# Two attentions and two expert feed forwards on one core: the feed forwards computed by routed slots, 85 tiles each, with gates and scatters placed inside the attentions

## The reference

```python
x = x + attn_a(_layernorm(x), ...)   # 8 heads of 128, relative positions, over all 1024 keys
x = x + ffn(_layernorm(x), ...)
x = x + attn_b(_layernorm(x), ...)   # 16 heads of 8 with one shared key and value head, causal
x = x + ffn(_layernorm(x), ...)      # the same weights again
```

```python
gate_scores = softmax(einsum('btd,ed->bte', x, Wg))
topk_val, topk_idx = top_k(gate_scores, 2)
topk_val = topk_val / (topk_val.sum(-1) + 1e-9)
comb = (one_hot(topk_idx, 8) * topk_val[..., None]).sum(-2)   # 4 x 1024 x 8, two entries per token not zero
for e in range(8):
    h = einsum('btd,hd->bth', x, W1[e]) + b1[e]               # 128 -> 512
    a, b = split(h, 2, axis=-1)
    eo = einsum('bth,dh->btd', a * sigmoid(b), Wo) + bo       # 256 -> 128, Wo and bo shared by the experts
    out = out + eo * comb[..., e:e+1]
```

## Time and profile before

| | |
|---|---|
| time, median of 3 runs | 2801.4 us (2800.65 to 2802.06) |
| profiled execution | 2800.0 us, span 2798.3 us, mean granted clock 0.967 |
| PE busy | 2620.7 us, 94% of the span |
| PEld busy | 2042.4 us, 73% |
| DVE busy | 2037.5 us, 73% |
| ACT busy | 1656.8 us, 59% |
| POOL busy | 385.7 us, 14% |
| chain that ended last | PE 80%, DVE 11%, ACT 5% |

### The profile page before, as it was taken

How to read it: one execution, slowest core, us unless ns; L and a number is a source line. 1 busy time by engine, 2 the same in 40 slices (tenths; PEclk the granted TensorE clock), 3 DMA queues, 4 the chain that set the end, 5 groups by cost and what they waited for, 6 DMA issues and landing times.

```text
span 2798.3 us, 45154 instructions
## 1 busy us (share of the span) xinstructions
PE 2620.7 (94%) x14496; PEld 2042.4 (73%) x14496; DVE 2037.5 (73%) x5225; ACT 1656.8 (59%) x3430; POOL 385.7 (14%) x813
## 2 busy tenths in 40 slices
PE   4999999999999999999999889989998989988998
PEld 3788788888888888888888667755555555545776
DVE  4677766767767777677776678878777777773887
ACT  3566666666666666665666445536666656655454
POOL 1000000000000000000110233402222212222344
PEclk8999999999999999999999989969999999998999
DMA  3665566566665666656666000000000000000000
GB/s 125 226 220 200 181 224 210 192 211 208 210 211 198 210 211 209 209 206 210 226 233 209 10 1 1 1 1 1 1 1 1 1 1 1 1 1 1 9 9 16
DMA packets 97587, 321.63 MB, mean 115 GB/s; under 512 B 11924, under 2 KB 25620, under 8 KB 97140
## 3 DMA queue, kind: packets, MB, share of 16 engines
q1 hardware_dynamic: 92650, 312.84, 32.6%
q0 software_dynamic: 1584, 4.33, 0.5%
q10 hardware_dynamic: 3120, 1.57, 0.2%
HBM read 158.53 MB, written 157.29 MB: 113 GB/s over the span
## 4 chain that ended last, share of the span: by engine, by line
PE 80%; DVE 11%; ACT 5%; issue 3%; POOL 1%; DMA 0%; SPq 0%; DVEq 0%; ACTq 0%; POOLq 0%
PE ps L243 8%; PE ps L245 7%; PE ps L244 7%; PE ps L630 7%; PE ps L743 5%; PE ps L605 5%; PE ps L604 5%; PE ps L781 5%; PE ps L643 4%; PE ps L645 4%; PE ps L644 4%; PE ps L763 4%; PE ps L675 4%; PE ps L676 4%; PE ps L677 4%
## 5 line engine op out<-in xcount | busy, mean ns | idle before, releaser
L910 ACT ACTIVATE a_Ph<-ps 128x512 fp32r<-128x512 f32 x512 | 305.9, 597 | 467.8 <-PE ps L630 467.7
L1215 DVE CUSTOM_DVE_ANT_0 a_sp<-ps,a_sp 128x1024 f32<-128x1024 f32 x256 | 313.2, 1223 | 180.0 <-PE ps L245 175.9
L980 ACT ACTIVATE r_P<-ps 128x512 f32<-128x512 f32 (+3 forms) x768 | 327.9, 491 | 187.1 <-PE ps L763 182.8
L1221 DVE TENSOR_TENSOR a_Pl<-ps,a_Ph 128x512 fp32r<-128x512 f32 x512 | 349.2, 682 | 10.0 <-ACT a_Ph L910 9.8
L604 PE MATMUL ps<-a_fa,a_ua 128*128 128x384 f32 (+2 forms) x960 | 327.2, 353 | 19.3 <-DVE a_fb L1176 13.9
L931 ACT ACTIVATE r_y<-ps 128x256 f32<-128x256 f32 x512 | 194.6, 385 | 216.6 <-PE ps L677 212.4
L903 ACT ACTIVATE a_sp<-a_sp,a_nm 128x1024 f32<-128x1024 f32 x256 | 295.0, 1152 | 32.1 <-DVE a_nm L1215 31.4
L630 PE MATMUL ps<-ident,a_sp 128*128 128x128 f32 x2048 | 309.0, 273 | 0.0
L743 PE MATMUL ps<-r_K,r_Q 128*128 128x512 f32 (+3 forms) x768 | 282.5, 403 | 18.2 <-DVE r_mx L1366 12.8
L630 PEld LDWEIGHTS ps<-ident,a_sp 128*128 128x128 f32 x2048 | 250.8, 141 | 61.7 <-issue 0.6
L605 PE MATMUL ps<-a_fb,a_ub 86*128 86x384 f32 (+2 forms) x960 | 290.8, 318 | 0.0
(11 more groups left out here) (217 smaller groups left out, 5676.0 us busy)
## 6 DMA issues: line engine op xcount, KB each, us to landing
scr<-a_rt SPq DMA_DIRECT2D x256, 576.0 KB, 3.1
a_sp<-scr SPq DMA_DIRECT2D x256, 512.0 KB, 4.4
a_wc<-wsp SPq DMA_DIRECT2D x24, 512.0 KB, 5.5
wsp<-a_wc SPq DMA_DIRECT2D x8, 512.0 KB, 5.6
a_ub<-a_ua SPq DMA_DIRECT2D x64, 44.0 KB
a_w1st<-in_w1t POOLq DMA_DIRECT2D x8, 256.0 KB, 4.6
out<-x SPq DMA_DIRECT2D x4, 512.0 KB, 3.2
a_w1r<-in_w1r POOLq DMA_DIRECT2D x8, 254.0 KB, 4.4
```

The source lines that it names most:

```text
L910: e.activation(self.Ph[:, n % 3, :], ps[:, 4 + n % 2, :], ACT.Copy).then_inc(S["p_hi"], 1)
L980: e.activation(self.P[:, pt, off:512], ps[:, bank, off:512], ACT.Exp).then_inc(S["b_exp"], 1)
L1215: e.tensor_tensor_reduce(out=w, in0=ps[:, 2:4, :].rearrange("p a n -> p (a n)"), in1=w, scale=-1.0, scalar=3e38, op0=ALU.add, op1=ALU.min, ...
L1221: e.tensor_tensor(self.Pl[:, n % 3, :], ps[:, 4 + n % 2, :], self.Ph[:, n % 3, :].bitcast(F32), ALU.subtract).then_inc(S["p_lo"], 1)
```

## The change

Each token is given two *slots*, one for each of its experts. The batches are taken in three parts, `PARTS = ((0, 1), (2,), (3,))`; within a part the slots of an expert stand together and are padded to whole tiles of 128, so that a part has `PT` = 39, 23 and 23 tiles whatever the routing is, 85 in a feed forward. They are loaded in groups of four tiles. The units are:

- `m_rank` for a batch, nine fp32 matmuls of 8 to 72 columns in one bank, and `m_slot` for a part, a chain of some 12 to 18 small instructions on VectorE: they count the tokens of each expert and give the slot of each token (`m_slot`) and the expert of each tile (`m_mapi`).
- `m_disp` for a token tile: VectorE makes the normalised row tile `m_xd` (two buffers), and GpSimd issues two indirect DMAs that scatter its 128 rows to their slots in a DRAM table `xsd`.
- `m_load` and `m_turn` for a group: SyncE loads four slot tiles, TensorE transposes them (L726), ScalarE and VectorE make the high and the low part.
- `m_mm` for a slot tile: TensorE reads the expert's number from memory into a register (once for up to eight tiles) and does the three matmuls against the weights that the register picks, over banks 0 to 3; ScalarE makes the hyperbolic tangent (the sigmoid in another form), VectorE the gated product `m_gg`; there is no factor for the token's weight here.
- `m_store` for two slot tiles: SyncE stores them to a DRAM table `gsd`. `m_gath` for a token tile: GpSimd issues two indirect DMAs that gather its rows of both experts into `m_gb` (three buffers). `m_sum`, `m_fin`, `m_proj`: the weighted sum of the two, its transposition and projection, the way out as before. `m_bias` adds bo times the sum of a token's weights to x, which stood in the way out before.

`plan_a` gets the gates, ranks and slots of batches 0 to 2, the scatters of parts 0 and 1 and their biases, and two loads. The expert weights are loaded and split earlier, in steps 52 to 68. 5.6 MB of DMAs on GpSimd's queue clear the slot tables once. Attention B's layer norm of batch 0, which stood in the first feed forward, goes into its opening, and `plan_b` gets those of batches 1 to 3 (those of 1 and 2 stood in the first feed forward), and the gates, ranks, slots and scatters of batches 0 to 2 for the second feed forward. `p_xh` and `p_xl` hold two batches instead of four. In `plan_f` the sums begin at tile 47 (`first`) and stand 2.6 tiles apart (`every`): 15 of them. The other 17 are in `rest`, which is dealt out over the opening of attention B after the first feed forward, and follows at the end after the second.

The diff, cut to what the above speaks of:

```diff
+PARTS = ((0, 1), (2,), (3,))
+PT = [2 * L // 128 * len(p) + E - 1 for p in PARTS]
+PG = [(t + 3) // 4 for t in PT]
+PP = [(t + 1) // 2 for t in PT]
...
+def at(counts, f, part):
+    return sum(counts) * f + sum(counts[:part])
+def place(f, b):
+    part = [b in p for p in PARTS].index(True)
+    return [("m_rank", f, b)] + ([("m_slot", f, part)] if b == PARTS[part][-1] else [])
+def disp(f, part):
+    return [("m_disp", f, n) for b in PARTS[part] for n in range(8 * b, 8 * b + 8)]
...
-            extra.setdefault(64 * b + 7 + i, []).append(it)
+        for i, it in enumerate(splits(1)(b - 1, 7) + gates(0, b - 1) + place(0, b - 1)):
+            extra.setdefault(64 * b + 6 + i, []).append(it)
+    for b, part in ((2, 0), (3, 1)):
+        for i, it in enumerate(disp(0, part) + [("m_bias", 0, c) for c in PARTS[part]]):
+            extra.setdefault(64 * b + 21 + i, []).append(it)
+    for g in range(2):
+        extra.setdefault(64 * 3 + 40 + g, []).append(("m_load", 0, 0, g))
...
+def plan_f(f, more):
+    groups = [(part, g) for part in range(3) for g in range(PG[part])]
+    side = {0: [("b_load",)] if f == 0 else [("m_bias", 1, 2)]}
+    ln = splits(2 * f + 1)(B - 1, 7)
+    for i, it in zip((1, 2, 3, 5, 6, 8), ln):
+        side.setdefault(i, []).append(it)
+    for i, it in enumerate(gates(f, B - 1) + [None] + place(f, B - 1) + disp(f, 2) + [("m_bias", f, B - 1)]):
+        side.setdefault(10 + i, []).append(it)
+    if f == 0:
+        side.setdefault(30, []).append(("b_zero", 0))
+        side.setdefault(34, []).append(("b_prepare",))
+    last = [sum(PT[:part + 1]) - 1 for part in range(3)]
+    for part in range(2):
+        side.setdefault(last[part], []).extend(("m_gath", f, n) for b in PARTS[part] for n in range(8 * b, 8 * b + 8))
+    back = [[u for u in (("m_sum", f, n), ("m_fin", f, n - 1, 5 + (n - 1) % 2), ("m_proj", f, n - 2, 7)) if 0 <= u[2] < NT]
+            for n in range(NT + 2)]
+    first, every = last[0] + 9, 2.6
+    p, i, nb = [("m_turn", f, 0, 0, 4), ("m_load", f, 0, 2)], 0, 0
+    for k, (part, g) in enumerate(groups):
+        for t in range(4 * g, min(4 * g + 4, PT[part])):
+            p.append(("m_mm", f, part, t, i % 4))
+            if t % 2 or t == PT[part] - 1:
+                p.append(("m_store", f, part, t // 2))
+            if t % 4 == 1 and k + 1 < len(groups):
+                p.append(("m_turn", f, *groups[k + 1], 4))
+                if k + 3 < len(groups):
+                    p.append(("m_load", f, *groups[k + 3]))
+            p += [u for u in side.pop(i, []) if u]
+            if i >= first + every * nb:
+                p += back[nb]
+                nb += 1
+            i += 1
+    p += [("m_gath", f, n) for n in range(8 * B - 8, 8 * B)]
+    rest = [u for its in back[nb:] for u in its]
+    if f == 0:
+        rest.append(("b_zero", 1))
+    return p + (spread(more, rest) if more else rest)
...
-    out = first(0) + prepare(0) + chain(0)
-    late, tail = splits(2)(B - 1, 7) + [("xb_bias", b) for b in range(B)], []
+    opening = splits(2)(0, 7) + first(0) + prepare(0) + chain(0)
+    out, late, tail = [], [("xb_bias", 0)], []
+    rows = disp(1, 0) + disp(1, 1)
+    rows_at = {(2, 1): rows[0:4], (2, 2): rows[4:8], (2, 3): rows[8:12], (3, 0): rows[12:16], (3, 1): rows[16:19],
+               (3, 2): rows[19:22], (3, 3): rows[22:24]}
...
+        for i, it in enumerate(rows_at.get((b, g), [])):
+            k = main.index(("b_s", b, g, 1, 3 - i // 2, 2 * (i % 2))) + 1
+            main.insert(k, it)
+            price.insert(k, 0)
         side = prepare(n + 1)[AHEAD:] + chain(n + 1) if n < 15 else []
-        side = spread(side, late, 9) if side else late
+        if g == 0 and b:
+            late += splits(3)(b - 1, 7) + gates(1, b - 1) + place(1, b - 1)
+        elif g == 1 and b + 1 < B:
+            late += splits(2)(b + 1, 7) + [("xb_bias", b + 1)]
+        elif g == 1:
+            late += [("m_bias", 1, c) for c in PARTS[0]]
+        half = len(side) // 2 if g == 1 else len(side)
+        side = spread(side[:half], late, 9) + side[half:] if side else late
         late = [("b_norm2", b, g, 1)]
         if g == 3:
             late += [(u, b, half) for half in range(2) for u in ("b_out", "b_out2")]
-        if g == 0 and b:
-            late += splits(3)(b - 1, 7) + gates(1, b - 1)
         total, goal, done, spent = sum(price), sum(cost(u) for u in side), 0, 0
         for i, u in enumerate(main):
...
+    def load_rows(self, e, u):
...
+        _, f, part, g = u
+        i, k = at(PG, f, part) + g, min(4, PT[part] - 4 * g)
+        if g == 0:
+            for s in range(2):
+                e.wait_ge(self.d_scat[s], 16 * (NT * f + 8 * PARTS[part][-1] + 8))
+        if i >= 2:
+            e.wait_ge(S["m_tr"], i - 1)
+        rows = self.xsd[part][512 * g:512 * g + 128 * k, :].rearrange("(k p) d -> p k d", p=128)
+        e.dma_start(self.sx[:, i % 2, 0:k, :], rows).then_inc(self.d_xs[i % 2], 16)
...
+        if u[0] == "m_disp":
+            _, f, n = u
+            i, part = NT * f + n, [n // 8 in p for p in PARTS].index(True)
+            e.wait_ge(S["m_xd"], i + 1)
...
+            for k in range(2):
+                e.indirect_dma_start(self.xsd[part], bass.IndirectOffsetOnAxis(self.slot[:, k, n:n + 1], 0),
+                                     self.xd[:, i % 2, :], None).then_inc(self.d_scat[i % 2], 16)
+        elif u[0] == "m_gath":
+            _, f, n = u
+            i, part = NT * f + n, [n // 8 in p for p in PARTS].index(True)
...
+            if i >= 3:
+                e.wait_ge(S["m_sum"], i - 2)
+            for k in range(2):
+                e.indirect_dma_start(self.gb[f][:, i % 3, k, :], None, self.gsd[part],
+                                     bass.IndirectOffsetOnAxis(self.slot[:, k, n:n + 1], 0)).then_inc(self.d_gath[i % 3], 16)
...
+        if u[0] == "m_rank":
+            _, f, b = u
...
+            e.wait_ge(*free[7])
+            e.matmul(ps[:, 7, 0:72], self.upper[:, :], self.both[:, :, :].rearrange("p n e -> p (n e)"), start=True, stop=False)
+            for n in range(8):
+                i = e.matmul(ps[:, 7, 8 * n + 8:72], self.ones[:, :], over(self.both[:, n, :], (0, 8 - n), (1, E)),
+                             start=False, stop=n == 7)
+            i.then_inc(S["m_rmm"], 1)
+            free[7] = S["m_rk"], r
...
+        elif u[0] == "m_mm":
+            _, f, part, t, bank = u
...
+            if t % 8 == 0:
+                n = min(8, PT[part] - t)
+                e.load(self.expert[t % 16:t % 16 + n], self.mapi[0:1, part, t:t + n])
+            if t % 4 == 0:
+                e.wait_ge(S["m_xlo"], at(PG, f, part) + t // 4 + 1)
+            e.wait_ge(*free[bank])
+            k, cs, hb = e.snap(self.expert[t % 16], min_val=0, max_val=E - 1), slice(128 * (t % 4), 128 * (t % 4) + 128), ps[:, bank, :]
+            wh, wl = (w[:, bass.ds(k, 1), :].rearrange("p k n -> p (k n)") for w in (self.Wh, self.Wl))
+            e.matmul(hb, self.sxh[:, s, cs], wh, start=True, stop=False)
+            e.matmul(hb, self.sxh[:, s, cs], wl, start=False, stop=False)
+            e.matmul(hb, self.sxl[:, s, cs], wh, start=False, stop=True).then_inc(S["m_mm"], 1)
+            free[bank] = S["m_gate"], i + 1
...
+        elif u[0] == "m_disp":
+            _, f, n = u
+            i, b = NT * f + n, n // 8
+            if i >= 2:
+                e.wait_ge(self.d_scat[i % 2], 32 * (i // 2))
+            e.tensor_scalar(self.xd[:, i % 2, 0:127], x[:, n, 0:127], self.mv[:, 1 + b, n % 8, 0:1], self.rs[:, 1 + b, n % 8:n % 8 + 1],
+                            ALU.subtract, ALU.mult).then_inc(S["m_xd"], 1)
+        elif u[0] == "m_bias":
+            _, f, b = u
...
+            e.wait_ge(S["m_xd"], NT * f + 8 * b + 8)
+            for n in range(8 * b, 8 * b + 8):
+                i = e.scalar_tensor_tensor(x[:, n, :], self.fbo[:, :], self.csum[:, n:n + 1], x[:, n, :], ALU.mult, ALU.add)
+            self.step(i)
...
+        elif u[0] == "m_mm":
+            _, f, part, t, bank = u
+            i, p = at(PT, f, part) + t, at(PP, f, part) + t // 2
+            e.wait_ge(S["m_sig"], i + 1)
+            if t % 2 == 0 and p >= 4:
+                e.wait_ge(self.d_gs[p % 4], 16 * (p // 4))
+            e.scalar_tensor_tensor(self.gg[f][:, p % 4, t % 2, :], self.sig[f][:, i % 4, :], 1.0, ps[:, bank, 0:FH], ALU.add,
+                                   ALU.mult).then_inc(S["m_gate"], 1)
```

715 lines of the change are left out of this document (397 added, 318 removed).

## The result

The changed kernel takes 2737.5 us (median of 4 runs, 2736.7 to 2737.8) against 2801.0 before: a ratio of 0.9773, 95% interval 0.9758 to 0.9788, 63.5 us faster. The profiled execution has a span of 2735.7 us, 62.6 less than the one before. The prediction was 2660 us, a gain of 139 to 141: the direction and the range (2580 to 2740) held, the gain was less than half of the forecast.

A forecast was written before the change was run, and what follows sets the result against it. TensorE's order of work was taken to bound nearly every stretch. First feed forward with opening -128, second feed forward -74, attention B +45, attention A +18 gave -139 us: 2660 us, range 2580 to 2740.

The forecast's parts named there:

- attention A: First attention: rank steps, slot chains and biases add 18 us, bounds 5 and 35; table-clearing copies counted as nothing.
- first stage: First feed forward's 85 expert tiles with 15 sums among them: 120 us, bounds 100 and 145.
- opening with 17 sums: Start of attention B with layer norm and 17 sums dealt out: 68 us, between 64 and 80.
- attention B: Rest of attention B: norms, ranks, slot chains, biases and normalised rows add 45 us, bounds 20 and 80.
- second stage: Second feed forward's 85 expert tiles, with eight more biases than the first: 122 us.
- tail: End of the second feed forward: 17 uncovered sums, 36 us, and 8 for the last sum, projection and store.
- What bounds the kernel, and the work removed: TensorE's work sets nearly every stretch; 85 tiles instead of 256 remove 120 us of matmuls per feed forward.
- the allowance of 13 us over TensorE's sum: In the second stage: 122 us taken against TensorE's 107, for VectorE standing for other engines and scatters.
- I cost them at nothing: Attention A: 5.6 MB of table-clearing copies cost nothing on DMA engines 60% busy, up to 8 us if row fetches come late.
- its pitch: Tail: each sum's two gathers through three buffers take 2.1 us around the ring, against GpSimd's 2.0.
- Rival 2: GpSimd's queue of 256 indirect DMAs is the bound at 2.0 us an issue: 2740 us; chance 0.11.
- The rule of the Trainium skill: GpSimd's DMA issues slow beside VectorE's two-port copies, 3100 ns instead of 620; for every issue, slower than before.

The follow-up runs named there:

- e0: Changed kernel unaltered, timed again in another session: 2697.2 us, ratio 0.9644 to the kernel before, no waits without a releaser on this core.
- e2: Changed kernel with the sums 1.7 slot tiles apart instead of 2.6 in both feed forwards: 2700.8 us, ratio 0.9640.
- e4: Changed kernel with each slot tile's expert a program constant, no register loaded, output of wrongly assigned experts: 2696.5 us, ratio 0.9617.
- e3: Changed kernel with the last batch's normalised rows and scatters at every second slot tile instead of every one: 2693.7 us, ratio 0.9610.
- e6: Changed kernel with the first feed forward's 17 left sums all done before attention B's opening, not dealt out over it: 2716.0 us, ratio 0.9707.
- e5: Changed kernel with batch 0's layer norm for attention B among the first feed forward's last slot tiles, not in the opening: 2698.6 us, ratio 0.9631.
- e1: Changed kernel with the slot tables cleared in eight pieces instead of four copies at once: 2691.0 us, ratio 0.9606.
- e9: Changed kernel with tables cleared in eight pieces and the last batch's rows at every second slot tile: 2728.6 us, ratio 0.9740; unaltered beside it 2743.2.
- e17: Changed kernel with tables cleared in pieces, last batch's rows at every second tile, sums 3.5 and 1.7 tiles apart: 2717.8 us; unaltered beside it 2740.6.
- e14: Changed kernel with all gathers and scatters plain DMAs of 128 rows in order, not computing the reference: 2675.4 us, ratio 0.9540.
- e12: Changed kernel unaltered, timed again as yardstick in another session: 2703.2 us, ratio 0.9651, no waits without a releaser on this core.
- e16: Same kernel as e14, all gathers and scatters plain, in another session: 2677.1 us, ratio 0.9550; the unaltered changed kernel beside it took 2740.6.
- e10: Changed kernel with each gather issued a second time into an unread buffer: 2898.2 us, ratio 1.0334; unaltered beside it 2743.2.
- e8: Changed kernel unaltered, on e0's chip 15 minutes apart: 2743.2 us, ratio 0.9778, 71 us of waits without a releaser on this core.

## Why the prediction was right in direction and wrong in size

The terms, with the result (upper level) and e0 (lower level), both against the earlier trace rows:

| term | predicted | result | e0 |
|---|---|---|---|
| attention A | +18 | +35.7 | +34.2 |
| first stage | 120 | 129.6 | 122.0 |
| opening with 17 sums | 68 | 98.5 | 95.0 |
| attention B | +45 | +38.6 | +28.0 |
| second stage | 122 | 131.6 | 120.8 |
| tail | 44 | 60.1 | 51.4 |
| sum | -139 | -62.6 | -105.3 |

Of the 76 us that the result is short, 43 are the upper level, which no term held. The other 34 are, at the lower level, the opening (27), attention A (16) and the tail (7), less 17 that attention B was priced too dear.

**What bounds the kernel, and the work removed.** Right. The trace has 170 expert tiles (L743) in the two stages together instead of 512, which by the prediction's 0.70 us a tile is 120 us of matmuls less in each.

**The stages.** Right at the lower level, to 2 us, but by errors that cancel in part: a sum costs 1.8 us there and not 1.2 (e2), the registers cost 2 us a stage (e4), standing for scatters 4 to 6 (e3), and the allowance of 13 us over TensorE's sum happened to cover them.

**The opening: the step that failed most.** "64 us if it never waits, 80 if nothing of it fills a gap; I take 68." It took 95.0 and 98.5, above the upper bound. The prediction added VectorE's work to VectorE's gaps, as if VectorE held the pace. But the earlier trace rows already has TensorE busy for 46.6 of the 53.6 us, at a clock of 0.59, against VectorE's 37.4, and the sum left its work out; with a norm and no sum at all the opening takes 64.4 us (e6). The result's trace in four parts:

```profile
1730.70:1748.00 17.30, 5.19 (x26) 4.15 (x25) 8.78 (x35) 4.74 (x10) 5.34 (x6) 0.64 0.26 80
1748.00:1766.00 18.00, 13.17 (x41) 8.89 (x40) 6.17 (x14) 12.78 (x23) 5.32 (x5) 0.50 0.10 30
1766.00:1797.00 31.00, 25.59 (x112) 20.01 (x112) 22.10 (x64) 7.64 (x19) 12.43 (x13) 0.77 0.20 58
1797.00:1829.20 32.20, 28.30 (x111) 22.63 (x110) 26.64 (x90) 7.66 (x17) 9.04 (x9) 0.61 0.12 35
```

In the first 35 us VectorE is busy for 15: norm, transposes, projection and keys follow on one another, and TensorE, which waits in between, has a clock of 0.50 to 0.64. In the last 63 it is busy for 48.7. In place of 68 the runs give 53.6 + 11 for the norm (11.4 by e5, 10.8 by e6) + 30.6 for the sums (e6) = 95. The norm had been put at 7. The sums had been put at 20 with most of that hidden in gaps; 18 of the 48.7 us that they take alone are hidden, and 30.6 stay. The last eight cost 1.2 each, the others 2.3 (e2, e6). That the chain of the first 35 us is what makes those dearer is argued from the four windows, not tested.

**Attention A: the step "I cost them at nothing".** The copies that clear the tables were put beside DMA engines that are 60% busy, with 8 us at worst. That is the mean of the stage; issued together, the copies filled the engines for 21 us, and the step that met them took 13 to 14 us more. In pieces 11 us come back over the steps concerned (e1), and attention A ends 7 to 15 us earlier (e1, e9, e17). The rest, 34 - 14 = 20 against 18, falls to ranks, slots, biases and scatters by subtraction; no run measured them.

**The tail.** The issue was right (0.97 us against 1.0), its pitch was not. In e0's tail, three issues of GpSimd and three sums of VectorE:

```profile
2662.58 0.96 POOL L662 DMA_INDIRECT m_gb<-gsd,m_slot  x1 [0.30 <-issue]
2663.84 0.95 POOL L662 DMA_INDIRECT m_gb<-gsd,m_slot  x1 [0.30 <-issue]
2665.10 0.95 POOL L662 DMA_INDIRECT m_gb<-gsd,m_slot  x1 [0.30 <-issue]
...
2663.38 0.48 DVE L1410 SCALAR_TENSOR_TENSOR m_acc<-m_gb,m_pw,m_acc 128x256 f32<-128x256 f32 x1 [1.54 <-ACT m_acc L1045]
...
2665.83 0.49 DVE L1410 SCALAR_TENSOR_TENSOR m_acc<-m_gb,m_pw,m_acc 128x256 f32<-128x256 f32 x1 [1.44 <-ACT m_acc L1045]
...
2668.41 0.48 DVE L1410 SCALAR_TENSOR_TENSOR m_acc<-m_gb,m_pw,m_acc 128x256 f32<-128x256 f32 x1 [1.56 <-ACT m_acc L1045]
```

Behind each issue stand 0.30 us, so a sum takes 2 x 1.26 = 2.52 us and not 2.1. 17 x 0.4 are 7 of the 7.4 us that the tail is over its 44. From issue to landing, put at 4.5 us by the earlier trace rows, it was 3.5 for a gather and 2.6 for a scatter (medians, e0), so the landing was not what set the pace.

**Attention B.** Predicted too dear: +28.0 at the lower level, inside the bounds of 20 and 80. e14 puts the standing for scatters there at 4 us at that level (703.2 against 707.6 in e12), where 6 were allowed for; that is hardly more than one kernel's own scatter (699.9 in e16). Which of the other terms were too dear no run tells.

**The upper level.** 42.7 us between e0 and the result that stood in no term and no rival. Rival 2 priced a slow issue in GpSimd's queue at 2740 us; the time came near it by another way, since the issue was not slow. Doubled gathers raise the late releases from 71 to 207 us (e10), and plain DMAs in order remove them (e16). It is not the chip (e0 and e8). By what path an indirect DMA holds back TensorE's releases, and why only in some sessions, stays open. Two hints. In the result's attention B, where indirect issues stand in seven places only, each late wait began within 1.4 us of the start of one. And the waits of attention B stand at the same places in both traces: ScalarE's exponentials (L1177) are let go late at 2271.25, 2457.32 and 2493.52 us in the result and at 2275.40, 2460.09 and 2496.25 in e8.

**The rule of the Trainium skill** that spoke against the change ("SBUF — State Buffer", section "SBUF: two separate sides", 3100 ns for a DMA overlapped with a copy-like instruction of VectorE) does not hold here as a price for every issue, which is how the prediction used it. Of 256 indirect issues the longest took 1.23 us, and of the 24 during which VectorE ran one of the normalised rows (L1380) none took over 1.02. Such a row takes 0.34 us, and no trace row tells its port mode, so no run here shows what a long copy would do.

## What to carry to other kernels

In a stretch whose engines are all idle in part, side work can cost more than the engine time it takes: here 30.6 us for 20.8 of VectorE's work in the sums, and 11.4 for 6.7 in the norm. Before giving its "gaps" to side work, look whether the engine is idle there because it waits for the same chain (here it was busy 15 of the first 35 us). Clear or copy large tables in pieces beside transfers that others wait for, and don't judge by the mean load: 5.6 MB at once held VectorE up for 14 us in a stage whose DMA engines are 60% busy in the mean, because for 21 us they were full; in eight pieces the same bytes cost 11 us less. And time a kernel that gathers or scatters by index in several sessions before believing a difference of under 2%.

## What the runs showed of the hardware that was not expected

- An indirect DMA of 128 rows holds GpSimd 0.96 to 0.97 us (medians of 128 gathers and 128 scatters of the result), with 0.30 behind it where they follow on one another; the plain one 0.54 (e16).
- With indirect DMAs under way ScalarE and VectorE can wait up to 4.9 us (e8) for results of TensorE, sometimes both let go at once: 53 to 71 us in a run of 2740 in three of five sessions with the changed kernel, none in the other two, none with plain DMAs in order (e16). One chip showed both.
- Matmuls whose weights are picked by a register cost 2 us more per 85 tiles than fixed ones (e4: 119.6 and 118.6 us a stage against 122.0 and 120.8 in e0).
